# Message-passing layers of a graph network on one core: two more of every 128 row tiles fetched row by row, issued by SyncE

## What is computed

```python
x_i = h[dst]
x_j = h[src]
hk = relu(concat([x_i, x_j]) @ linA_w[l].T + linA_b[l])
w = sigmoid(hk @ linB_w[l].T + linB_b[l])
prop = segment_sum(w * x_j, dst, num_segments=N)
emb = relu(concat([h, prop]) @ lin_w[l].T + lin_b[l])
```

## Time and profile before

| | us |
|---|---|
| median of 3 runs | 11612.29 |
| lowest, highest run | 11603.48, 11631.40 |
| span of the profiled execution, first to last instruction of the program | 8105.0 |
| POOL busy in it | 5899.4 |
| DVE, PE, ACT busy in it | 4894.9, 4794.9, 1394.6 |
| HBM traffic in it | 1025.41 MB read, 45.47 MB written |

### The profile page before, as it was taken

The page is one execution under the profiler, slowest core; times in us unless marked ns, Lnnn a source line. Parts: engine busy times, 40 slices in busy tenths (PEclk is TensorE's granted clock), DMA queues, the critical chain, the costliest instruction groups (busy, mean ns, idle before and its releaser), DMA issues.

```text
span 8105.0 us, 161654 instructions
## 1 busy us (share of the span) xinstructions
PE 4794.9 (59%) x26657; PEld 4101.0 (51%) x26658; DVE 4894.9 (60%) x25933; ACT 1394.6 (17%) x5213; POOL 5899.4 (73%) x6246
## 2 busy tenths in 40 slices
PE   6888888888755555555565555555546555555555
PEld 5777777777544444444444444444445444444444
DVE  6777778777655555555555555555555555555555
ACT  3333333333300000000020000000011000000002
POOL 6777777777477777777757777777766777777775
PEclk6555555555655555555565555555556555555555
DMA  5444444444444444444454444444445444444443
GB/s 160 132 132 132 131 131 132 132 131 131 127 134 132 132 132 134 132 132 134 132 154 132 132 132 134 132 132 134 132 116 168 132 132 134 132 132 133 132 132 104
DMA packets 638944, 1078.97 MB, mean 133 GB/s; under 512 B 324360, under 2 KB 399016, under 8 KB 637772
## 3 DMA queue, kind: packets, MB, share of 16 engines
q0 software_dynamic: 296832, 810.95, 34.5%
q1 hardware_dynamic: 306076, 247.79, 10.3%
q10 hardware_dynamic: 35156, 12.72, 0.7%
HBM read 1025.41 MB, written 45.47 MB: 132 GB/s over the span
## 4 chain that ended last, share of the span: by engine, by line
POOL 30%; issue 23%; ACTq 14%; PE 12%; DMA 9%; DVE 7%; ACT 2%; DVEq 2%; POOLq 1%; SPq 0%
POOL G L783 29%; ACTq L1027 10%; DMA G<-mp_rows,idx 5%; PE ps L1816 4%; DMA G<-gat_rows,idx 2%; ACTq L1024 2%; PE ps L1778 2%; ACTq L1026 2%; DMA acc<-in_src 1%; PE ps L1813 1%; PE ps L1805 1%; DVE junk L1605 1%; ACT gate L1018 1%; PE ps L1916 1%; DVEq L1212 1%
## 5 line engine op out<-in xcount | busy, mean ns | idle before, releaser
L783 POOL DMA_INDIRECT G<-mp_rows,idx x4404 | 4165.4, 946 | 1490.4 <-issue 1279.1
L1916 PE MATMUL ps<-selw,G 128*128 128x32 f32 x8808 | 2077.6, 400 | 634.0 <-DVE selw L1614 626.5
L1916 PEld LDWEIGHTS ps<-selw,G 128*128 128x128 f32 x8808 | 1960.5, 328 | 894.9 <-issue 859.3
L1594 DVE TENSOR_TENSOR pen<-ps,G 128x512 f32<-128x512 f32 x1101 | 760.8, 691 | 2476.0 <-DMA G<-mp_rows,idx 2464.2
L1906 PE MATMUL ps<-awin,ring 96*128 96x128 bf16 x4692 | 713.7, 307 | 2160.3 <-DVE ring L1578 2148.0
L783 POOL DMA_INDIRECT G<-gat_rows,idx x1564 | 1488.8, 952 | 491.9 <-issue 442.3
L1906 PEld LDWEIGHTS ps<-awin,ring 96*128 96x128 bf16 x4692 | 413.5, 133 | 2309.3 <-DVE ring L1578 2305.3
L881 ACT COPY idx<-idx_all 128x4 int32 (+1 forms) x1568 | 299.7, 192 | 4716.5 <-issue 4500.7
L1605 DVE SCALAR_TENSOR_TENSOR junk<-pen,ps 128x128 f32<-128x128 f32 x4692 | 1057.2, 278 | 0.1
L1578 DVE TENSOR_TENSOR ring<-ring,ps 96x512 bf16<-96x512 bf16 x1173 | 792.3, 675 | 40.0 <-DMA ring<-rel_dst 40.0
L1816 PE MATMUL ps<-sel,weighted 128*128 128x32 f32 x3128 | 748.9, 404 | 0.0
(11 more groups left out here) (206 smaller groups left out, 5188.7 us busy)
## 6 DMA issues: line engine op xcount, KB each, us to landing
acc<-mp_rows ACTq DMA_DIRECT2D x9216, 1.0 KB
ring<-rel_dst SPq DMA_DIRECT2D x294, 384.0 KB
G<-mp_rows,idx POOLq DMA_INDIRECT x4404
ring<-rel_dst SPq DMA_DIRECT2D x98, 512.0 KB
awin<-mp_dst_rows SPq DMA_DIRECT2D x1173, 24.0 KB
G<-gat_rows,idx POOLq DMA_INDIRECT x1564
mp_rows<-acc SPq DMA_DIRECT2D x36, 512.0 KB, 3.0
mp_dst_rows<-acc SPq DMA_DIRECT2D x36, 384.0 KB, 5.2
```

What stands on the lines that cost most here:

```text
L783: pool.indirect_dma_start(out=to[:, t, :], out_offset=None, in_=table, in_offset=bass.IndirectOffsetOnAxis(ap=idx[:, T * u + t:T * u + t + ...
L1594: v.tensor_tensor(pen[:, off % 2, :].rearrange("p (t c) -> p t c", t=T), PS[off % 2][:, :].rearrange("p (t c) -> p t c", t=T), slot(k0, of ...
L1916: i = mm(PS[2 + off % 2][:, 0:W], slot(k0, off)[:, t, 0:D], selw[:, off % 4, W * t:W * t + W], start=(t == 0), stop=(t == T - 1))
```

## The change

`FAR` and `NEAR` get one more group each: 21 (lane 2) and 5 (lane 3). Their single rows are issued by SP, in the same pattern that ACT uses for lanes 0 and 1: `fetch_ids`, `slot_and_ids` and `eight_rows` of SP's own, with eight registers (`sp_rows`) and a semaphore of its own (`sp_ids_in`). SP's loop has bodies of 32 groups in place of 8, and reads the window bases every eight groups as before. Ahead of the loop SP waits for the store of `T1`. The nine semaphores of the attention block named above become two counters (`tops`, `al`), on which each step waits for five or four times the group's number; this makes room for the new ones. `LANES` becomes 4, which makes `lone` and `lone_ids` larger and adds four semaphores `rows_in`.

```diff
-FAR = {19: 0}
-NEAR = {3: 1}
+FAR = {19: 0, 21: 2}
+NEAR = {3: 1, 5: 3}
...
+        sp_ids_in = sem("sp_ids_in")
...
-                    "selT sel pen sjT mx dg mxs ma hi r1 mid r2 e8s den den4 rhs e8 mnew dd mkept ex ex4 "
-                    "ee R nd tt acc").split()}
-        gat_sems["al"] = [sem(f"gat_al{n}") for n in range(4)]
+                    "selT sel pen sjT mx dg mxs tops e8s den den4 rhs e8 mnew dd mkept ex ex4 "
+                    "ee R nd tt acc al").split()}
...
+            sp_rows = [sp.alloc_register(f"sp_row{n}") for n in range(ROWS)]
+
+            def load_starts(k0, lo=0):
+
+                sp.load(sp_regs, base_sb[0:1, bass.ds(k0 + lo, U)])
...
-                def body(k0, stop=U):
-                    starts = load_starts(k0)
+                def eight_rows(n, part):
+
+                    lo = ROWS * part
+                    sp.load(sp_rows, lone_ids[:, P * n + lo:P * n + lo + ROWS])
+                    for m, reg in enumerate(sp_rows):
+                        node = sp.snap(reg, min_val=0, max_val=N - 1)
+                        sp.dma_start(lone[lo + m:lo + m + 1, n, T - 1, :],
+                                     T1[bass.ds(node, 1), :]).then_inc(rows_in[n][l // 2], 16)
+
+                def fetch_ids(n, k0, at):
+                    with nc.allow_non_contiguous_dma(reason="every fourth edge"):
+                        sp.dma_start(lone_ids[:, P * n:P * n + P], lone_sources(k0, at)).then_inc(sp_ids_in, 16)
+
+                def slot_and_ids(k0, off, earlier, ids):
+                    if reached(k0, off, V):
+                        sp.wait_ge(mp["agg"], km + k0 + (earlier + 1))
+                        sp.sem_inc(waited, 1)
+                    sp.wait_ge(sp_ids_in, l * (V * BODIES) + k0 + ids)
+                    sp.sem_inc(waited, 1)
+
+                def lone_rows(k0, off):
+                    if off == 0:
+                        if reached(k0, off, 1):
+                            eight_rows(NEAR[5], 15)
+                        if not (isinstance(k0, int) and k0 == LAST):
+                            fetch_ids(FAR[21], k0, 21)
+                    elif off <= 16:
+                        if off == 1:
+                            slot_and_ids(k0, off, 21 - V, 16)
+                        eight_rows(FAR[21], off - 1)
+                        if off == 16:
+                            fetch_ids(NEAR[5], k0, 5 + V)
+                    else:
+                        if off == 17:
+                            slot_and_ids(k0, off, 5, 32)
+                        eight_rows(NEAR[5], off - 17)
+
+                def body(k0, stop=V):
                     for off in range(stop):
+                        if off % U == 0:
+                            starts = load_starts(k0, off)
                         if off % 4 == 0:
                             offsets(k0, off)
-                        window(k0, off, starts[off])
-
+                        window(k0, off, starts[off % U])
+                        if stop == V or off == 0:
+                            lone_rows(k0, off)
+
+                sp.wait_ge(t1_out, 16 * NQ * (l + 1))
                 body(0)
-                with sp.Fori(1, NG // U - 1) as turn:
-                    body(turn * U)
+                with sp.Fori(1, BODIES) as turn:
+                    body(turn * V)
                 body(LAST, REST)
...
             def gat_hi(k0, off, done=gat):
-                dve.wait_ge(done["ma"], k0 + (off + 1))
-                v.tensor_copy(sm16[:, off % 4, 0, :], sm[:, off % 4, 0, :]).then_inc(done["hi"], 1)
+                dve.wait_ge(done["tops"], 5 * k0 + (5 * off + 1))
+                v.tensor_copy(sm16[:, off % 4, 0, :], sm[:, off % 4, 0, :]).then_inc(done["tops"], 1)
```

More of the change, by code:

```diff
@@ L640, in _ @@
             sp_regs = [sp.alloc_register(f"sp_base{n}") for n in range(U)]
-            def load_starts(k0):
-                sp.load(sp_regs, base_sb[0:1, bass.ds(k0, U)])
+            sp_rows = [sp.alloc_register(f"sp_row{n}") for n in range(ROWS)]
+            def load_starts(k0, lo=0):
+                sp.load(sp_regs, base_sb[0:1, bass.ds(k0 + lo, U)])
                 return [sp.snap(reg, min_val=0, max_val=N - 1) for reg in sp_regs]
@@ L718, in offsets @@
                     to, of = offsets_of_four(k0, off, S * W)
-                    sp.dma_start(to, of).then_inc(offs_in[off // 4], 16)
+                    sp.dma_start(to, of).then_inc(offs_in[off // 4 % 2], 16)
                 def window(k0, off, start):
@@ L1287, in gat_rhs @@
                     dve.wait_ge(done["e8"], k0 + (off - 1))
-                dve.wait_ge(done["r2"], k0 + (off + 1))
+                dve.wait_ge(done["tops"], 5 * k0 + (5 * off + 5))
                 m = sm[:, off % 4, :, :]
@@ L1298, in gat_e8s @@
                 if reached(k0, off, 2, done):
-                    dve.wait_ge(done["al"][3], k0 + (off - 1))
+                    dve.wait_ge(done["al"], 4 * k0 + (4 * off - 4))
                 dve.wait_ge(done["e8"], k0 + (off + 1))
@@ L1313, in gat_al0 @@
                 v.tensor_tensor(a[:, 0, :, :], e[:, :, 0:H], Grows[:, off % U, :, D:D + H],
-                                ALU.add).then_inc(done["al"][0], 1)
+                                ALU.add).then_inc(done["al"], 1)
             def gat_al1(k0, off, done=gat):
                 a = al[:, off % 2, :, :]
-                dve.wait_ge(done["al"][0], k0 + (off + 1))
+                dve.wait_ge(done["al"], 4 * k0 + (4 * off + 1))
                 v.scalar_tensor_tensor(a[:, 1, :], a[:, 0, :], SLOPE, a[:, 0, :], ALU.mult,
-                    ALU.max).then_inc(done["al"][1], 1)
+                    ALU.max).then_inc(done["al"], 1)
             def gat_al2(k0, off, done=gat):
                 e, a = views(off)
-                dve.wait_ge(done["al"][1], k0 + (off + 1))
-                v.tensor_tensor(a[:, 2, :, :], a[:, 1, :, :], e[:, :, H:2 * H], ALU.min).then_inc(done["al"][2], 1)
+                dve.wait_ge(done["al"], 4 * k0 + (4 * off + 2))
+                v.tensor_tensor(a[:, 2, :, :], a[:, 1, :, :], e[:, :, H:2 * H], ALU.min).then_inc(done["al"], 1)
             def gat_al3(k0, off, done=gat):
                 e, a = views(off)
-                dve.wait_ge(done["al"][2], k0 + (off + 1))
-                v.tensor_tensor(a[:, 3, :, :], a[:, 2, :, :], e[:, :, H:2 * H], ALU.subtract).then_inc(done["al"][3], 1)
+                dve.wait_ge(done["al"], 4 * k0 + (4 * off + 3))
+                v.tensor_tensor(a[:, 3, :, :], a[:, 2, :, :], e[:, :, H:2 * H], ALU.subtract).then_inc(done["al"], 1)
             def gat_mnew(k0, off, done=gat):
```

16 lines of the change are left out of this document (8 added, 8 removed).

## The result

The kernel after takes 12634.74 us (median of 4 runs, 12617.96 to 12658.31), the kernel before on the same chip 11611.85 us (11603.48 to 11631.4): ratio 1.088, 95% interval 1.0867 to 1.0894. Forecast were 11525 us and a range of 11470 to 11590. The prediction was wrong in sign and by 1110 us. It chose the wrong side between its forecast and rival B.

What follows compares the result with a forecast made beforehand. The prediction took the number of gathers POOL issues as the bound: 72 fewer save 90 us, layer starts cost 3, so -87 us from 11612.3 gives 11525 us, with a range of 11470 to 11590.

Steps and rivals of the forecast that it cites:

- rival B: SP's loop, eight rows between two windows, becomes the bound: +462 us at the upper bound per row, 12074 us; chance 0.09.
- SP's 4.51 us a group: SP's loop: rows, register load, window, offsets and bases sum to 4.51 us, hidden behind POOL's 4.84 at no cost.
- The margin of 0.33 us: SP's loop: time to spare per group, 7%, against POOL's mean group of 4.84 us after the change.
- What bounds: POOL: the number of gathers it issues bounds the kernel, at 1.25 us a tile.
- the -90 us: POOL in the message layers: 72 gathers fewer at 1.25 us each, counted in full as 90.0 us saved.
- the 3507 us: Median of the runs above the profiled span of 8105 us; unexplained by any row, taken as constant for the forecast.
- Rival A: Whole kernel: runs without the profiler are uniformly slower by 1.43, so the gain is 125 us, 11487 us; chance 0.13.
- rival E: Time outside the span grows with the longer program; growth above 87 us makes it slower; chance 0.04.
- deciding point of 4.84 us: SP's loop: SP becomes the bound above 4.84 us a group, a row of 0.255 us.
- rival C: POOL's gathers slow from extra traffic; 15 ns each eats the gain, about 11612 us; chance 0.08 together with no effect.
- the DMA side: Queues: 9216 more 1 KB rows move from q0 to q1, no more bytes in all; cost 0.
- about +830 us: SP's register load: at the skill's 200 ns per register, SP needs about 5.6 us a group; rejected for the trace.

Runs made afterwards that it cites:

- plain transfers: Kernel after, POOL's message-layer gathers replaced by transfers of 128 fixed rows: 9603.76 us, 0.8135; the same edit in the kernel before: 8732.15 us, 0.7401.
- the fill of 0.222 us: Kernel before without any single rows, POOL filling a 128 x 128 scratch tile behind every gather: ratio 0.8922.

## Why the prediction was wrong

**The step that failed first: SP's 4.51 us a group.** It decided between the forecast and rival B, and it was too short even for an undisturbed SP. With plain transfers SP needs 5.26 us, counted over 320 groups of a layer: rows 3.46 to 3.49 us by layer, each instruction with the gap behind it, where 3.15 + 0.16 stood (the row's DMA itself is 0.228 us, near the 0.22 taken; the gaps were too short); the load of eight registers 0.73, where 0.53 stood; the window 0.59, not 0.48; offsets 0.13, not 0.12; bases with their registers, loop turns, fetches and waits some 0.3, not 0.07. The register load was priced by L644, once in eight groups; L732 behind a window is 0.717 us in the median, which is ACT's 0.722 and not SP's 0.526. The margin of 0.33 us was 7%, and five terms each missed in the same direction. With 5.26 in the prediction's own formula for rival B, 391 x 3 x 5.26 = 6170 us against 5790: +380 us, slower, and that without any slowed instruction, as in the profile of before.

**The second: what bounds.** "The kernel is bound by the number of gathers that POOL issues" holds for the execution in the profile, and for no run of before or after. In the runs of before ACT's row loop sets the pace (period 7.00 us, 4.88 in the profile), in those of after SP's (7.90), and a gather less gives next to nothing: the -90 us, 0.8%, measured as about 0.3%.

**The third: the 3507 us.** "No row says what lies in that. If it is constant" was the sentence to stop at. A median 43% above the span means that the profile and the runs are not the same thing, and then every "which engine is last" read from it is open. Here the added time was stalls inside the span. Rival A took the factor as uniform, rival E as growth outside; it was neither: the stalls are on the two sequencers that the change was about to load.

**Rival B** named the place, the mark in the waits and the sign. Its price, +462, was too low: the periods give (7.90 - 7.00) x 391 x 3 = 1056 us, against 1023 measured. Its deciding point of 4.84 us was POOL's group, and the runs' was ACT's loop.

**Right were** the merged semaphores, the longer bodies, the gathers' 945 to 946 ns beside more rows (rival C falls), and the DMA side: q1 7.1% and q0 22.3% of the 16 engines' time in after. For the two places on the Trainium skill: its figure of about 200 ns for a register in a load (Runtime: NRT & Kernel Launch, Instruction fetch mechanics) stays too high, 0.73 / 8 = 0.09 us here. What the prediction worked out from that figure as an estimate, about +830 us, does not come out of its own formula, which gives (4.51 - 0.53 + 1.60) x 391 x 3 - 5790 = +755. Its sentence that issuing from several engines saves sequencer time "which is usually small" beside the DMA itself (DMA: Bandwidth & Descriptors, Issuing engines are not separate DMA queues) is no guide here, but in the other direction than the prediction had it: 1152 groups of rows on SP cost 8.8% and those on ACT 10.7%, because sequencer time was the bound.

**Left open:** why the recorded profile had no slow instructions with gathers 1.25 us apart. It was one execution; the condition did not come again in any run. So the gathers at that distance are not enough by themselves, and what else it takes is not known. By what path POOL's gathers reach the other sequencers is not shown either, only that they do. Recording the trace does not seem to be it: the profiled run of before took 11659.88 us, the seven beside it 11628.58 to 11651.05.

## What to carry to other kernels

When the median of the runs lies far above the profiled span, first profile again, and argue only from an execution whose time is that of the runs. Count a sequencer's loop instruction by instruction with the gaps behind each, take every duration from the same neighbours that it will have, and don't rest a forecast on a margin of 7%. Single-row transfers with a register address are paid in sequencer instructions (a load, and three instructions each), so where that sequencer also issues what others wait for, a gather by indices can be the cheaper form: without any single rows POOL was busy 57% of the time and the kernel 10.7% faster.

## What the runs showed of the hardware

- In all profiles but one that have gathers by indices 1.25 us apart in the layers, other sequencers are slowed: register instructions of 29 to 44 ns take about 0.7 us on ACT and SP from some 4 to 5 us into a burst until about its end. The exception is the recorded profile of before, with none at the same distance. POOL's own are not slow there (0 of 3009), but with the fill of 0.222 us 94 of 8737 are. Plain transfers of the same size by POOL don't do it (in the layers of after the 1260 register instructions of over 300 ns on ACT and the 2134 on SP become 0 and 0).
- Work put between gathers can make a kernel faster: 2.7 ms of fills on POOL took before from 1.000 to 0.8612. The attention block, which has no single rows, gained too: 1564 gathers from 70 to 3074 us before, from 64 to 2522 us with the fill of 0.437 us.
- Results seem to reach a waiting engine late in such stretches too. In the attention block of after, where no single rows are issued, DVE's L1343 reads what PE's L1836 made. The profile has that matmul end at 999.14 us (its ends are modelled), and PE's last one before the pause, of the next group, at 1000.07; the semaphore that L1836 raises is recorded at 1006.57, and DVE went on at 1006.66, with POOL's gathers between. Such waits of DVE (`e <- remote`) come to 1183.4 us in before, 144.6 us in before with spaced gathers, and none in its recorded profile. The timeline of the one, and the row of the waits of the other two:

```profile
998.98 1.09 PE L1820 MATMUL ps<-ident,G 128*128 128x128 f32 x4
...
1003.85 0.95 POOL L825 DMA_INDIRECT G<-gat_rows,idx  x1 [0.30 <-issue]
1006.66 0.26 DVE L1343 TENSOR_REDUCE e<-ps 128x32 f32<-128x96 f32 x1 [7.39 <-remote]
```

```profile
DVE e L1301 <- remote: 1183.4, 193, 13.1
```

```profile
DVE e L1307 <- remote: 144.6, 62, 3.0
```

- The Trainium skill (Perfetto Trace Analysis, DMA Optimizations) says that balancing transfers over the issuing engines may help where an engine's track is full of descriptor generation. POOL's track looks like that in the recorded profile of before, 73% busy. It did not help here: moving the last tile of 72 more groups to SP lost 8.8%, and pausing POOL gained 13.9%.
